# An expert stage that fetches rows by token number and adds weighted rows into the output by DMA, in place of padded row copies and a combine stage

## The reference

```python
x = layernorm(L0_attn_x)                     # B=4, S=512, H=512: 2048 tokens
out = L0_attn_x + time_and_channel_mix(x)    # the "attn" block, RWKV-like
              + attention_then_moe(x)        # the "ffn" block
# inside attention_then_moe, after causal attention:
xn = rmsnorm(x, w_ln2)
logits = xn @ Wr.T                            # 8 experts
top_logits, top_idx = top_k(logits, 2)
probs = softmax(top_logits)
y_e = Wd[e] @ (silu(Wg[e] @ xn) * (Wu[e] @ xn))   # inner size 1024
moe = sum over the 2 chosen experts of probs * y_e
```

## Time and profile before

| | before |
|---|---|
| median of 3 runs | 2184.49 us (2183.06 to 2185.43) |
| profiled execution, first to last instruction (its own time) | 2181.5 us, 3.0 below the median of the runs |
| PE busy | 1906.3 us, 87% |
| DVE busy | 1211.0 us, 56% |
| ACT busy | 935.3 us, 43% |
| POOL busy | 376.7 us, 17% |
| DMA | 324.77 MB, 149 GB/s over the span |
| granted TensorE clock, mean | 0.915 of full |

### The profile page before, as it was taken

The page is one execution under the profiler, slowest core; times in us unless marked ns, Lnnn a source line. Parts: engine busy times, 40 slices in busy tenths (PEclk is TensorE's granted clock), DMA queues, the critical chain, the costliest instruction groups (busy, mean ns, idle before and its releaser), DMA issues. The chain is left out here.

```text
span 2181.5 us, 30371 instructions
## 1 busy us (share of the span) xinstructions
PE 1906.3 (87%) x10850; PEld 1633.6 (75%) x10850; DVE 1211.0 (56%) x1827; ACT 935.3 (43%) x1505; POOL 376.7 (17%) x391
## 2 busy tenths in 40 slices
PE   3878677899899899769999988999999999999980
PEld 2666455676676777658888868999999999999980
DVE  6886335726726636465555575555555555555544
ACT  4454333624525516422222215555555555555540
POOL 3233220010010100135000031111111111111115
PEclk9899886996987988889999998999999999999995
DMA  4664352260270261284020126555655555555527
GB/s 172 196 203 152 140 161 49 78 162 13 77 174 0 86 147 40 78 310 175 22 87 7 39 97 255 199 212 195 232 205 210 218 209 212 192 217 210 217 78 231
DMA packets 93795, 324.77 MB, mean 149 GB/s; under 512 B 8569, under 2 KB 25209, under 8 KB 75442
## 3 DMA queue, kind: packets, MB, share of 16 engines
q1 hardware_dynamic: 79122, 286.91, 38.7%
q0 software_dynamic: 6208, 20.98, 2.8%
q10 hardware_dynamic: 8416, 16.25, 1.9%
HBM read 232.47 MB, written 66.21 MB: 137 GB/s over the span
## 5 line engine op out<-in xcount | busy, mean ns | idle before, releaser
L46 PE MATMUL bank<-ex_x_hi,ex_w_hi 128*128 128x256 f32 x1472 | 419.4, 285 | 4.9 <-issue 4.9
L48 PE MATMUL bank<-ex_x_hi,ex_w_lo 128*128 128x256 f32 x1472 | 417.7, 284 | 0.0
L47 PE MATMUL bank<-ex_x_lo,ex_w_hi 128*128 128x256 f32 x1472 | 417.7, 284 | 0.0
L1148 DVE TENSOR_TENSOR ex_w_lo<-ex_stage,ex_w_hi 128x2048 fp32r<-128x2048 f32 x138 | 238.4, 1755 | 172.2 <-ACT ex_w_hi L1090 169.2
L46 PEld LDWEIGHTS bank<-ex_x_hi,ex_w_hi 128*128 128x128 f32 x1472 | 283.5, 193 | 7.9 <-issue 5.3
L47 PEld LDWEIGHTS bank<-ex_x_lo,ex_w_hi 128*128 128x128 f32 x1472 | 283.7, 193 | 2.7
L48 PEld LDWEIGHTS bank<-ex_x_hi,ex_w_lo 128*128 128x128 f32 x1472 | 283.5, 193 | 0.0
L1073 POOL TENSOR_TENSOR ex_a_lo<-ex_a,ex_a_hi 128x256 fp32r<-128x256 f32 x184 | 132.4, 742 | 679.1 <-ACT ex_a_hi L1110 679.1
L1105 ACT ACTIVATE ex_gate<-bank 128x256 f32<-128x256 f32 x184 | 70.5, 383 | 197.5 <-PE bank L48 197.5
L1926 PE MATMUL bank<-at_k,at_q 96*128 96x512 f32 (+3 forms) x256 | 115.2, 545 | 35.8 <-DMA at_k<-at_ones 24.5
L46 PE MATMUL bank<-ex_w_hi,ex_a_hi 128*128 128x512 f32 x368 | 144.3, 392 | 0.0
(11 more groups left out here) (254 smaller groups left out, 4338.9 us busy)
## 6 DMA issues: line engine op xcount, KB each, us to landing
ex_stage<-in_w_moe SPq DMA_DIRECT2D x69, 1536.0 KB, 6.3
first_w<-in_w_moe SPq DMA_DIRECT2D x23, 1536.0 KB, 6.5
scratch_tiles_in<-tm_zeros SPq DMA_DIRECT2D x4, 2944.0 KB, 17.3
scratch_tiles_out<-ex_y ACTq DMA_DIRECT2D x23, 512.0 KB, 3.3
at_q<-at_q_hi SPq DMA_DIRECT2D x32, 256.0 KB, 5.1
at_k<-at_k_hi SPq DMA_DIRECT2D x32, 256.0 KB, 6.4
cm_stage<-in_w_cm SPq DMA_DIRECT2D x8, 1024.0 KB, 8.2
first_x<-scratch_tiles_in SPq DMA_DIRECT2D x12, 512.0 KB, 6.9
```

What stands on the lines that cost most here:

```text
L46: pe.matmul(out, lhsT=w_hi, rhs=x_hi, start=first, stop=False)
L47: pe.matmul(out, lhsT=w_hi, rhs=x_lo, start=False, stop=False)
L48: return pe.matmul(out, lhsT=w_lo, rhs=x_hi, start=False, stop=last)
L1148: return dve.tensor_tensor(dst, src, hi.bitcast(F32), ALU.subtract)
```

## The change

Nothing of the matrix work changes. The padded copies `tiles_in` and `tiles_out`, the zero fill and `combine_phase` go.

- The router computes three more small tensors on DVE (`sub`, `within`, `places`) after `slots`, and POOL fills a table (`pairs_on_pool`): 32 small indirect DMAs write the pair (token number, weight) of each slot into `scratch_table`, 8 bytes a row, and SP loads the table back. A slot with no pair keeps a number of 2048 or more and weight 0.
- In the experts phase POOL fetches tile n+2 by two indirect gathers of 128 rows straight from `rows_in` (`fetch`); numbers of 2048 or more are skipped.
- SP stores the whole of `acc` to `out` at the start of the experts phase (four DMAs of 1 MB), and POOL waits for it (`base_out`) before its loop.
- ACT and DVE multiply by the slot's weight where they copied, and POOL adds the two 128-row halves of `y` into `out` by two indirect DMAs with `compute_op=ALU.add` (`add_rows`), after the adds of the tile before have landed. `out` has 256 more rows than tokens, which take the padding.

```diff
@@ time_mix_phase, SP
-                sp.dma_start(d["tiles_in"].rearrange("r h -> (r h)").rearrange(
-                    "(b n p e) -> b p n e", b=B, n=ZERO_PARTS, p=P)[b],
-                    zeros[:, :].unsqueeze(1).to_broadcast([P, ZERO_PARTS, ZEROS])).then_inc(w_in, 16)
@@ channel_mix_phase, POOL
             pool.memset(acc[:, :, :], 0.0).then_inc(route.consts, 1)
+            route.pairs_on_pool(pool)
+            pool.dma_start(d["table"].rearrange("(p s) w -> p s w", p=P), route.fill[:, :, :]).then_inc(table_filled, 16)
             pool.wait_ge(route.step, route.SLOTS)
-            with pool.Fori(0, B) as b:
-
-                pool.dma_start(rows[:, :, :], d["rows_in"][b].rearrange(tokens, p=P)).then_inc(rows_loaded, 16)
...
+            pool.wait_ge(table_filled, 16)
+            for b in range(B):
                 for j in range(TT):
                     for n in range(2):
                         pool.indirect_dma_start(
-                            out=d["tiles_in"], out_offset=bass.IndirectOffsetOnAxis(ap=route.now[:, n, j:j + 1], axis=0),
-                            in_=rows[:, j, :], in_offset=None).then_inc(sent, 16)
-                pool.wait_ge(sent, b * 32 * TT + 32 * TT)
+                            out=d["table"], out_offset=bass.IndirectOffsetOnAxis(ap=route.places[:, n, b, j:j + 1], axis=0),
+                            in_=route.pair[:, n, b, j, :], in_offset=None).then_inc(sent, 16)
@@ Router.on_dve
+        step(dve.tensor_scalar(self.sub[:, :, :, :], self.slots[:, :, :, :], 7, None, ALU.logical_shift_right))
+        step(dve.tensor_scalar(self.within[:, :, :, :], self.slots[:, :, :, :], P - 1, None, ALU.bitwise_and))
+        step(dve.scalar_tensor_tensor(self.places[:, :, :, :], self.within[:, :, :, :], float(SUBS), self.sub[:, :, :, :],
+                                      ALU.mult, ALU.add))
@@ experts_phase, SP
-                sp.wait_ge(turned, n + 1)
-                sp.dma_start(x_in[p][:, :, :],
-                             d["tiles_in"][bass.ds(n * TILE, TILE), :].rearrange(rows, p=P)).then_inc(x_loaded[p], 16)
...
+            for b in range(B):
+                sp.dma_start(d["out"][b * S:(b + 1) * S, :].rearrange(tokens, p=P),
+                             acc[:, b * TT:(b + 1) * TT, :]).then_inc(base_out, 16)
@@ experts_phase, POOL
+            def fetch(n, p):
+                pool.tensor_copy(fetch_at[:, p, :, :], table[:, bass.ds(n * TP, TP), :]).then_inc(fetch_at_ready, 1)
+                pool.wait_ge(fetch_at_ready, n)
+                pool.tensor_tensor(idle[:, 1:2], idle[:, 0:1], idle[:, 0:1], ALU.add)
+                for j in range(TP):
+                    pool.indirect_dma_start(
+                        out=x_in[p][:, j, :], out_offset=None, in_=rows_in,
+                        in_offset=bass.IndirectOffsetOnAxis(ap=fetch_at[:, p, j, 0:1], axis=0),
+                        bounds_check=TOKENS - 1, oob_is_err=False).then_inc(x_loaded[p], 16)
+
+            def add_rows(n, p, last):
+                pool.wait_ge(y_by_act, n + 3)
+                pool.wait_ge(y_by_dve, n + 3)
+                pool.wait_ge(y_out, n * 16 * TP + 32 * TP)
+                pool.tensor_tensor(idle[:, 1:2], idle[:, 0:1], idle[:, 0:1], ALU.add)
+                for j in range(TP):
+                    pool.indirect_dma_start(
+                        out=d["out"], out_offset=bass.IndirectOffsetOnAxis(ap=add_at[:, p, j, 0:1], axis=0),
+                        in_=y[:, p, j, :], in_offset=None, compute_op=ALU.add).then_inc(y_out, 16)
...
             def turn(it, last):
                 for g, n, p, c in slots(it, last):
                     if not (last and c == C - 1):
                         low(g + 1, c + 1)
-
+                    if c == C - 1:
+                        add_rows(n, p, last)
+                        if not last:
+                            pool.wait_ge(turned, n + 3)
+                            fetch(n + 2, p)
+
...
             low(0, 0)
+            pool.wait_ge(base_out, 16 * B)
@@ experts_phase, ACT (DVE alike, with tensor_scalar)
-                        act.activation(y[:, p, 0, :], y_bank(p, 0)[:, :], ACT.Copy).then_inc(y_by_act, 1)
-                        act.wait_ge(y_by_act, n + 3)
-                        act.wait_ge(y_by_dve, n + 3)
-                        act.dma_start(d["tiles_out"][bass.ds(n * TILE, TILE), :].rearrange(rows, p=P),
-                                      y[:, p, :, :]).then_inc(y_out[p], 16)
+                        act.activation(y[:, p, 0, :], y_bank(p, 0)[:, :], ACT.Copy,
+                                       scale=weight(p, 0)).then_inc(y_by_act, 1)
@@ build
-        experts_phase(nc, psum, ident[:, :], routing, first_tile, d)
-        combine_phase(nc, routing, acc, d)
+        experts_phase(nc, psum, ident[:, :], routing, first_tile, acc, d)
```

More of the change, by code:

```diff
@@ L865, in sem @@
             return ctx.enter_context(nc.semaphore("rt_" + nm))
[L867 removed]
+        self.experts = routing[1]
         self.rank_bank, self.total_bank = rank_bank, total_bank
@@ L870, in __init__ @@
         self.rows_in = self.raw[:, :, :]
-        self.now = sb("now", [P, 2, TT], mybir.dt.int32)
+        self.pair = sb("pair", [P, 2, B, TT, 2], I32)
+        self.fill = sb("fill", [P, SUBS, 2], I32)
+        self.slots = sb("slots", [P, 2, B, TT], I32)
+        self.sub = sb("sub", [P, 2, B, TT], I32)
+        self.within = sb("within", [P, 2, B, TT], I32)
+        self.places = sb("places", [P, 2, B, TT], I32)
         self.before = sb("before", [P, P], BF16)
@@ L986, in experts_phase @@
     assert TILES % 2 == 1
-    experts = routing[1]
+    table, experts = routing
     first_x, first_w, gain = first_tile
@@ L1026, in experts_phase @@
         y_by_dve = sem("y_by_dve")
-        y_out = [sem(f"y_out{p}") for p in range(2)]
+        y_out = sem("y_out")
+        base_out = sem("base_out")
+        fetch_at_ready = sem("fetch_at_ready")
+        add_at_ready = sem("add_at_ready")
+        filled = sem("filled")
         up_bank = psum[0:CK]
@@ L1084, in _ @@
             turn(TURNS, True)
+            pool.wait_ge(y_out, (TILES + 2) * 16 * TP)
+            for p in range(2):
+                pool.wait_ge(x_loaded[p], (TURNS + 1 - (1 - p)) * 16 * TP)
         @block.scalar
```

165 lines of the change are left out of this document (76 added, 89 removed).

## The result

| | before | changed kernel |
|---|---|---|
| median of 4 runs | 2183.77 us (2180.64 to 2185.43) | 2163.87 us (2163.11 to 2164.27) |
| ratio | | 0.9911, 95% interval 0.9898 to 0.9925 |
| span of the profiled execution | 2181.5 us | 2161.7 us |

The account below looks back on a forecast made before the run. Matmuls were taken to bound the experts phase and POOL's issuing the combine phase; -50.7 + 1.1 + 0.4 = -49.2 us took the span from 2181.5 to 2132.3, plus 3.0 for runs: 2135.3 us, range 2128 to 2150.

Parts of the forecast that it names:

- What bounds the kernel: Experts phase: matmuls alone set the time from 1317 to 2121 us; combine phase: POOL's rate of issuing gathers.
- Removed: the combine phase: End of the program: it ends with the last tile's adds, at 2130.8 instead of 2181.5, -50.7 us.
- my bound of -48.9: End of the program: smallest gain allowed for removing the combine phase, its range being -51.7 to -48.9 us.
- Added: POOL's work per tile: End of each experts tile: two adds, two gathers and small copies take 6.3 us, all hidden, cost 0.
- 5.4 us of cover: Experts phase, per tile: extra POOL time that stays hidden before DVE's product needs the `low` pair, 0.7 + 4.7 us.
- Added: the store of `acc`: Start of the experts phase: 4 x 1 MB behind the stage loads delay `low` of step 1, +1.1 us, bounds 0 and 12.
- One bound: Upper end of the forecast's own range, 2139: the store of `acc` at 271 GB/s was counted as 1.9 us more.
- Router: Channel mix start: DVE's second weight copy may stand behind POOL's five small fills, +0.4 us; or up to 2.4 us won.
- The step that failed: Router, channel mix: the table's 32 DMAs at 1.28 us replace larger ones on POOL; PE won't wait, no cost.
- the last step of the sum: From profiled span to measured runs: 2132.3 us plus 3.0, as runs stood above the span by the median, gives 2135.3.

Follow-up runs that it names:

- e12: As e2, with the adds into the output written as plain scatters, the addition left out; span 2138.5 us.
- e1: Changed kernel, with POOL waiting after each eight pair scatters until they have landed; span 2140.5 us.
- e2: Changed kernel, with the 32 pair scatters issued only after half of the channel mix turns; span 2139.3 us.
- e13: Changed kernel, with the table's DRAM tensor eight times as large, only its first 48 KB used and no instruction changed; span 2146.2 us.
- e16: Changed kernel, with POOL waiting for the last load of x before the first pair scatter; span 2139.5 us.
- e11: As e2, with the wait for the store of acc moved to before the first adds; 2138.82 us, ratio 0.9796.
- e5: Changed kernel, with the fetch ahead of the wait for a tile's result, and the wait for the store of acc before the first adds; span 2163.2 us.
- e6: Changed kernel, with four small POOL fills, each waited for, ahead of the 32 pair scatters; span 2155.4 us.
- e7: Changed kernel, with the table declared first of the DRAM scratch tensors, so at another address; span 2160.9 us.
- e18: The same program as e11 again, on chip 7 beside the unedited changed kernel; 2161.03 us, ratio 0.9898.
- e8: Changed kernel with 16 of the 32 pair scatters, those of each token's second expert left out; span 2134.6 us.
- e3: Changed kernel, with scatter rows of 64 bytes instead of 8, the table 393 KB; span 2141.2 us.
- e4: Changed kernel, with rows of 8 bytes written 64 bytes apart, the table 393 KB; span 2141.4 us.

## Why the prediction was wrong

- **What bounds the kernel.** Right. PE set the time of the experts phase, POOL's gathers that of the combine phase.
- **Removed: the combine phase.** Right in kind and 4.0 us too large: -46.7 instead of -50.7, outside my bound of -48.9. Of the 4.0, 2.95 lie in the landing. I had said "I take the gather and half of the 2.0 us of a 256 KB store, 6.5 us" and kept 8.3 as a bound; it was 9.4 (9.85 less the 0.4 to the end), and a plain scatter (e12) took longer still. The nearest row was the scatter's 8.3, not the gather's 5.5. The other 1.0 us is POOL's: 0.62 for an adding DMA (1.6 us instead of 1.0), 0.36 for its start.
- **Added: POOL's work per tile.** The cost of 0 was wrong by 2.6 us, the 1.7 and 0.9 of the waits shown above that are not the store's. I had priced both adds at the 1.3 us of the gathers before, which have no split of weights beside them; they take 1.6 and 2.6, the second beside DVE's split, as a plain scatter does too (e12). In the tile before the last one the work from POOL's one-element operation (2121.21) to the second fetch's end (2130.1) is 8.9 us, not 6.3. That uses 2.6 of the 5.4 us of cover, which still hides it. In one tile near 2050 us PE waits all the same. There DVE's split starts at 2049.86, just ahead of the first add instead of behind its start, and that add holds POOL for 3.64 us:

```profile
2050.01 3.64 POOL L1118 DMA_INDIRECT out<-ex_y,ex_add_at  x1 [1.46 <-issue]
...
2056.72 2.77 POOL L1107 DMA_INDIRECT ex_x_in<-scratch_rows_in,ex_fetch_at  x1 [0.58 <-issue]
```

  The fetch behind it comes late, and PE waits 1.74 us for its rows at 2067. With plain scatters (e12) none is longer than 2.6 us, and these waits are gone.
- **Added: the store of `acc`.** Right: POOL went on at 1362.14, which is 1339.0 in the time of the kernel before (its first `turn_x` was 23.16 us earlier), against 1339.1; PE lost 0.8 us there against 1.1. (In runs without the stall it lost 1.8 to 1.9, in e1, e2, e13 and e16, and nothing in e11, which has the wait elsewhere.) One bound was summed wrongly: at 271 GB/s the store adds 15.5 - 13.1 = 2.4 us, not 1.9; nothing hangs on it.
- **Router.** Right within what can be seen: channel mix without the stall takes 377.6 to 378.0 us in the runs with all scatters and no larger fill, against 377.9 before, so that +0.4 can't be told from 0. The two copies, now written with a stride, still stand until POOL's memset of `acc` is done, 4.34 us against 4.44:

```profile
936.71 4.34 DVE L947 COPY rt_pair<-rt_raw 128x16 f32<-128x16 f32 x2
```

- **The step that failed** is one that I passed over in a sentence: "The table's 32 DMAs at 1.28 us follow on POOL where 32 larger ones and three waits of 5 to 8 us for loads stood; PE doesn't wait there before and won't." The term stood at 0 and measured +22.5 us of channel mix: 14.2 of idle PE and 8.3 of matmuls at the lower clock. I looked at who waits for POOL's scatters, found nobody, and took that for no cost. The three pauses that the change removes, which I had named myself, were not weighed at all (whether they are what matters is not shown, see below). No row of before shows such a stall, though its combine phase issues 32 gathers in a row; there PE has nothing to do, so that it could not be seen.
- **What is shown of the cause.** On the chip of the first result, on 14 and on 7, all runs with 32 scatters without a pause (the changed kernel twice, e5, e6, e7, e18) stall PE, ACT and DVE, from 20 to 30 us after the first scatter until 3 to 5 us after the last. 16 of them don't (e8, chip 14). Neither their place in channel mix (e18), nor the address of the table (e7), nor full queues (e18) matter, and no transfer of code lies in the stall of e18. On chips 2, 3 and 12 nothing stalls.
- **What stays open.** Why it is there in some groups and not in others: chip and group can't be told apart. By what path POOL's scatters slow down the instructions of the other engines. Whether the stall exists when nothing is recorded: every run of the changed kernel and of the experiments on record comes with a span and a clock from a profile, and none is there without, so that the recording itself is not ruled out as a part of it. Whether a pause every eight scatters (e1) or larger or spread rows (e3, e4) help on a chip that stalls was not tried, since these ran on a chip that doesn't. e8 and the kernel before, which pauses after each eight and never stalled on chips 14 and 7 (2180.93 in one run and 2184.23 in the median of seven), speak for the pause; that is an argument and no measurement.

Without the stall the change is worth some 41 to 44 us: e1, e2 and e16, with one added wait each, measured 2142.22, 2141.08 and 2141.27, where the kernel before had 2183.57, 2183.57 and 2184.98. e13, whose instructions are those of the changed kernel, has 37.0 (2148.01 against 2184.98). All four are single runs. The forecast's 2135.3 misses the first three by 6 to 7 us. By spans it is more, 7.0 to 8.2 (2139.3 to 2140.5 against 2132.3), of which some 4 are the tail's and 2.6 the experts phase's in e2. The difference comes from the last step of the sum: I put the runs 3.0 us above the span, which compared the span of one execution with the median of others, and the runs on record lie 1.8 above their own span (2163.49 and 2161.7 in the changed kernel). That 1.2 us ran in the forecast's favour by luck. The range of 2128 to 2150 holds these runs; it didn't hold what the change cost where it stalls.

## What to carry to other kernels

Work that nobody waits for can still cost: ask of each moved or added run of DMA instructions not only who waits for it, but how long it goes on without a pause beside busy engines, and keep such runs short (16 cost nothing in e8, 32 cost 18 to 25 us on two of the five chips whose number is known). Count in such a loss also what PE does more slowly when it comes back: here 8.3 of 22.5 us. When an edit, and then an unlike one, both make a stall vanish, run the unedited kernel beside them before believing either. Price a DMA of POOL beside the work that will run beside it: the same scatter took 1.0 us alone and 2.6 beside DVE's split. And take the landing of the last transfer from the row of the same kind of transfer: a scatter's, not a gather's or a store's.

## What the hardware did that I had not expected

- A run of more than some 20 us of indirect DMAs from POOL (128 rows of 8 bytes each, one every 1.27 us) slows PE to an instruction each 0.7 us or a multiple of it and leaves ACT idle for 20.88 us and DVE for 12.61, with DMA engines at 0.02 of their time, on two of five chips. The same program differs by 22 us between two chips (2138.82 and 2161.03, four runs each), while the kernel before differs by 1.4 (2182.80 and 2184.23).
- An adding indirect DMA of 128 rows of 2 KB holds POOL for 1.6 us where a plain one takes 1.0. Started beside DVE's split of weights, either takes 2.6 us, and an adding one took 3.64 once. It lands no later than the plain one: 9.6 against 10.8 us from its start to the program's end.
